# Moving one subtraction per attention item from VectorE to GpSimd in a two-layer transformer kernel

## The reference

```python
# layer 0, attention: 32 query heads, 8 key/value heads of 64, sliding window of 64
qkv = einsum('bsd,od->bso', x, w_qkv)
q, k = rms_norm(q) * q_norm_w, rms_norm(k) * k_norm_w
q, k = rope(q, k)
scores = einsum('bhqd,bhkd->bhqk', q, k_rep) * HEAD_DIM ** -0.5 + sliding_mask
attn = einsum('bhqk,bhkd->bhqd', softmax(scores), v_rep)
out = einsum('bso,do->bsd', attn, w_out)
# layer 0, ffn: weights are int32 with a scale per row, 704 hidden
down(silu(gate(x)) * up(x))
# layer 1: full attention with 16 heads of 16, a rotation of the first 8 channels, no causal mask;
# and a feed-forward block that only the 64 best-ranked tokens of each sequence pass through
```

## Time and profile before

| | before |
|---|---|
| median of 3 runs | 1004.89 us |
| profiled execution | 1006.06 us, its span 1004.3 us |
| TensorE, VectorE busy | 915.7 us, 849.8 us |
| ScalarE, GpSimd busy | 662.2 us, 625.0 us |
| granted TensorE clock | 0.98 of full speed, mean |

### The profile page before, as it was taken

The page is one execution under the profiler, slowest core; times in us unless marked ns, Lnnn a source line. Parts: engine busy times, 40 slices in busy tenths (PEclk is TensorE's granted clock), DMA queues, the critical chain, the costliest instruction groups (busy, mean ns, idle before and its releaser), DMA issues. The chain is left out here.

```text
span 1004.3 us, 26048 instructions
## 1 busy us (share of the span) xinstructions
PE 915.7 (91%) x8671; PEld 500.2 (50%) x8671; DVE 849.8 (85%) x1760; ACT 662.2 (66%) x1747; POOL 625.0 (62%) x891
## 2 busy tenths in 40 slices
PE   4678999999998998999998997599999999999998
PEld 2455666766766766765766765242222222222223
DVE  6898889789789788888888886679999999999961
ACT  3655656556556555555655654128999999998985
POOL 4566668678678678668677766513776676454320
PEclk9899999999999999999999999789999999999999
DMA  7556555444445555445444544332312312413001
GB/s 240 120 100 134 113 95 97 96 93 95 97 90 99 97 86 99 97 92 97 98 88 95 89 87 90 104 92 68 69 27 26 47 27 48 75 40 53 20 5 43
DMA packets 253114, 83.60 MB, mean 83 GB/s; under 512 B 227317, under 2 KB 251573, under 8 KB 252725
## 3 DMA queue, kind: packets, MB, share of 16 engines
q1 hardware_dynamic: 249284, 76.43, 38.2%
q10 hardware_dynamic: 3696, 5.51, 2.0%
HBM read 18.49 MB, written 4.19 MB: 23 GB/s over the span
## 5 line engine op out<-in xcount | busy, mean ns | idle before, releaser
L1342 DVE TENSOR_REDUCE l_mxv<-l_mx 128x1 f32<-128x1024 f32 x256 | 295.0, 1216 | 19.5 <-PE l_mx L1562 19.1
L1262 ACT ACTIVATE l_prob<-l_sc 128x512 f32<-128x512 f32 x512 | 278.3, 598 | 18.3 <-PE l_sc L1570 15.5
L763 POOL TENSOR_TENSOR tt<-tt 128x320 f32<-128x320 f32 x128 | 110.4, 863 | 156.8 <-DVE tt L681 156.8
L420 ACT ACTIVATE an<-an 128x256 f16<-128x256 f32 x128 | 53.4, 417 | 231.9 <-DVE an L616 231.9
L1516 PE MATMUL l_acc<-l_prob,qkv_all 128*17 128x256 f32 x2048 | 161.0, 387 | 2.9 <-DVE l_acc L1325 0.5
L1562 PE MATMUL l_mx<-early 48*128 48x512 f16 x512 | 156.8, 388 | 4.2 <-DVE l_ones L1288 2.6
L754 POOL TENSOR_TENSOR rm<-ss,half_neg 128x5 f32<-128x5 f32 x128 | 159.8, 1248 | 0.0
L1570 PE MATMUL l_sc<-early 50*128 50x512 f16 x512 | 154.8, 383 | 0.1
L884 PE MATMUL qk<-early,xh 128*128 128x384 f16 x512 | 127.9, 332 | 4.8 <-DVE early L565 4.7
L937 PE MATMUL ob<-wo_hi,ats 128*128 128x256 f16 x512 | 105.7, 274 | 6.0 <-DMA ats<-an 4.5
L681 DVE TENSOR_TENSOR tt<-qk,tcw 128x640 f32<-128x640 f32 x128 | 104.4, 816 | 3.7 <-ACT v L420 1.6
(11 more groups left out here) (184 smaller groups left out, 1938.9 us busy)
## 6 DMA issues: line engine op xcount, KB each, us to landing
qkv_all<-w_qkv SPq DMA_DIRECT2D x3, 768.0 KB, 9.2
v<-v SPq DMA_DIRECT2D x64, 32.5 KB, 1.9
xn_all<-xs SPq DMA_DIRECT2D x16, 128.5 KB, 2.1
xa<-x SPq DMA_DIRECT2D x16, 128.0 KB, 2.3
tk<-nat SPq DMA_TRANSPOSE x128, 2.8
qkv_all<-w_o ACTq DMA_DIRECT2D x8, 256.0 KB, 3.1
ats<-an SPq DMA_TRANSPOSE x128, 2.4
xc<-x SPq DMA_DIRECT2D x16, 128.0 KB, 2.3
```

The source lines that it names most:

```text
L420: return act.activation(dst, src, ACT.Copy, scale=scale)
L763: pool.tensor_tensor(t1[:, b, :, :].rearrange("p h (a d) -> p h a d", a=2), t1[:, b, :, :].rearrange("p h (a d) -> p h a d", a=2), tt[:, b ...
L1262: act.activation(prob[:, (y * NI + u) % NPR, h * 512:(h + 1) * 512], sc[:, k % NSC, :], ACT.Exp, scale=D1 ** -0.5).then_inc(s_["act_sc"], 1)
L1342: dve.tensor_reduce(mxv[:, x % 2, u:u + 1], mx[:, MX[k] % 2, :], AX.X, ALU.max).then_inc(s_["dve_mx"], 1)
```

## The change

The subtraction for the low parts of the four queries (`nat[:, b, 2:NB, HD:P]`) leaves VectorE, where it stood behind the key's subtraction at lag 6, and is now issued by GpSimd at lag 5, between the rotation's addition and the power of the item that follows. It waits for ScalarE's high parts (`act_hi`) and, before it writes into `nat`, for the DMA that last read this buffer. What waited for the semaphore `dve_ql` now waits for `pool_lo`: SP's transposing DMA and VectorE's product L681, two items later.

```diff
@@ sync @@
                     sp.wait_ge(s_["dve_kl"], m + 1)
-                    sp.wait_ge(s_["dve_ql"], m + 1)
+                    sp.wait_ge(s_["pool_lo"], m + 1)
@@ vector, at(s, LAG_K) @@
                     dve.tensor_tensor(nat[:, b, 1, 0:HD], t1[:, b, 0, :], nat[:, b, 0, 0:HD], ALU.subtract
                                       ).then_inc(s_["dve_kl"], 1)
-                    dve.wait_ge(s_["act_hi"], n * G + k + 1)
-                    dve.tensor_tensor(nat[:, b, 2:NB, HD:P], t1[:, b, 1:NH, :], nat[:, b, 2:NB, 0:HD], ALU.subtract
-                                      ).then_inc(s_["dve_ql"], 1)
@@ vector, at(s, LAG_A) @@
+                    wait(dve, s_["pool_lo"], n * G + k - 1)
                     wait(dve, s_["dve_kl"], n * G + k - 1)
-                    wait(dve, s_["dve_ql"], n * G + k - 1)
@@ gpsimd, between the rotation's addition and the power @@
+                n, k, ok = at(s, LAG_N)
+                b = k % 2
+                if ok:
+
+                    pool.wait_ge(s_["act_hi"], n * G + k + 1)
+                    landed(pool, n * G + k - 2)
+                    pool.tensor_tensor(nat[:, b, 2:NB, HD:P], t1[:, b, 1:NH, :], nat[:, b, 2:NB, 0:HD], ALU.subtract
+                                       ).then_inc(s_["pool_lo"], 1)
```

More of the change, by code:

```diff
@@ L275, in layer0 @@
                  "act_sq act_A act_kh act_hi act_th act_kc act_kt act_exp act_an act_xh act_xat act_l1 "
-                 "dve_A dve_ss dve_a dve_h dve_rc dve_an dve_al dve_kl dve_ql dve_xl "
+                 "dve_A dve_ss dve_a dve_h dve_rc dve_an dve_al dve_kl dve_xl "
                  "dve_b1 dve_g1 dve_v1 dve_xn dve_x1 dve_b2 dve_g2 dve_v2 dve_xs dve_wr dve_b3 dve_v3 "
                  "dve_xa dve_raw dve_top dve_rest "
-                 "pool_rm pool_u pool_v pool_rs1 pool_rs2 pool_tcw pool_xa "
+                 "pool_rm pool_u pool_v pool_lo pool_rs1 pool_rs2 pool_tcw pool_xa "
                  "pool_r1 pool_r2 pool_rope pool_ones act_wq dve_wq act_wo dve_wo dve_gu dve_wd set_dve set_pool set_k").split()
```

## The result

The changed kernel takes 1010.5 us (median of 22 runs, 1006.63 to 1025.27); the kernel before took 1004.79 in 22 runs beside it. The ratio is 1.0062, 95% interval 1.004 to 1.0084. The profiled execution of the changed kernel took 1011.56 us. In some executions of these kernels TensorE's granted clock stays at 1.2 GHz for 37.5 us between the two layers (e2's trace, from 646.5 us on) and not for 14 us (before, from 647.6 on), which costs about 12 us; so beside the times I compare how far layer 0 has come: the start of the probability matmuls (pv) of item 12 and of item 124, seven periods of 16 items later.

The account below looks back on a forecast made before the run. TensorE was taken as near its limit, with VectorE a second bound alternating within each period. 6.7 periods x (-1.4 + 0.5) = -6.0, head +1, layer 1 and tail 0: -5 us, 1000 on the median; range 992 to 1015.

Parts of the forecast that it names:

- What goes: VectorE loses 128 subtractions, 0.35 us per item; two runs of busy items per period, taken as -1.4 us a period.
- What comes: GpSimd gets 128 subtractions of 0.73 us each (bounds 0.55 and 0.86), making it 89% busy per period.
- rival 3: Shared SBUF port: the key's subtraction on VectorE is held behind GpSimd's new one; +22 us, 1026; chance 0.07.
- The head: From 20 to 100 us, VectorE splitting weights: -4.2 us relief, +5 for blocked weight instructions; taken as +1 us.
- the price of the late place: Behind the layer-1 rotation, once per period, GpSimd runs two microseconds late: +1.0 us, 0.5 absorbed, +0.5 net.
- Mostly ScalarE has room for that: ScalarE's two copies to nat come 0.73 us later per item, claimed mostly harmless as the copy stands last, behind exp.
- three of four items per period stay on time: Argument against rival 1: by the prediction's sums, lateness on GpSimd stays confined to the remaining items of a period.
- About +1.0 us at that sc: TensorE's scores behind the layer-1 rotation: two subtractions add 1.5 us, up to 0.4 taken back; 0.5 then absorbed.
- The moved waits: tk's transpose and VectorE's product two items later now wait for GpSimd; claimed free on time, late only behind the layer-1 rotation.
- Rival 2: Late transposes queue on SP, so the output projection (ob) gets its input up to 1.9 us later; +9, 1014; chance 0.18.
- Rival 1: The place behind the layer-1 rotation costs 1.2 us a period and eats the gain; 1005 to 1006; chance 0.22.
- The sign for "wrong": The prediction would be wrong if, among other signs, the transposes become TensorE's longest wait.

Follow-up runs that it names:

- e2: The changed kernel with the subtraction moved only for items with m % 16 under 12, the others kept on VectorE; 1003.8 us, ratio 1.0006 to the kernel before.
- e3: The kernel before with the queries' subtraction left out on every engine; 990.3 us, ratio 0.9846.
- e17: The kernel before without VectorE's subtraction; GpSimd does it into an unread buffer, tk not waiting, only for items m % 16 under 12; 998.2 us.
- e1: The changed kernel with the subtraction moved only for items with m % 16 of 12 and more; 1012.6 us, ratio 1.0059 to the kernel before.
- e18: The kernel before without VectorE's subtraction; GpSimd does it into an unread buffer, tk not waiting, only for items m % 16 >= 12; 994.6 us.
- e5: The kernel before without VectorE's subtraction; GpSimd does it for all items into an unread buffer and tk's transpose does not wait; 1007.8 us.
- e13: e5 with ScalarE's copy of the carried keys issued one slot earlier, ahead of the copy to nat; 1012.0 us, ratio 1.0041 to the kernel before.
- e6: The changed kernel with GpSimd's subtraction ahead of the rotation's addition; 1037.6 us, ratio 1.0314 to the kernel before.
- e9: e5 with GpSimd's subtraction behind the scaling, not ahead of the power; 1055.3 us, ratio 1.0489 to the kernel before.
- e10: The changed kernel with the moved subtraction behind the next item's scaling; 1069.5 us, ratio 1.0594 to the kernel before.
- e8: The kernel before with the layer-1 rotation's three GpSimd instructions spread over three successive items; 1003.6 us, ratio 0.9964 to the kernel before.
- e14: The changed kernel with ScalarE's copy of the carried keys issued one slot earlier, ahead of the copy to nat; 1017.7 us, ratio 1.0113 to the kernel before.

## Why the prediction was wrong, step by step

It forecast 1000 us, five less than before; the kernel takes five to six more. The range (992 to 1015) holds the time, but its middle rests on a price that failed.

- **"What goes"** was right in sum, by luck. The forecast's relief is 6.7 x 1.4 + 4.2 = 13.6 us, e3 shows 13.57. By place it was off: 1.86 a period (13.03 / 7) and not 1.4, and 0.5 in the head and not 4.2.
- **"What comes", the duration**: 0.72 us against 0.73. L667 (now L664), taken as unchanged, fell by 0.06, and L645 (now L642), which stood only in rival 3, by 0.26.
- **The head**, put at +1: 2.95 by the traces, with the lower clock named above. Its +5 was 8 x 0.65 us of held weight instructions. No run shows the 0.65: for instance the eight instructions that write `wo_lo` rose by 0.10 each (0.76 to 0.86 us), and in e3, with nothing new on GpSimd, by 0.12.
- **The step that failed is the price of the late place**, +1.0 us a period, 0.5 after absorption, with the load on GpSimd at nothing elsewhere. Load and wait cost 2.2 us a period there (the change less e3 in the four items: 2.16 + 0.07), 1.95 of them the load; the net came to +2.16 and not +0.5, while the rest of the period gave 1.52, near the forecast's 1.4. (With the stretch taken one or two items earlier the net is 1.6 or 1.4, and load and wait still cost 2.2 or 2.3.) With the +5 in the head the forecast had 8.4 us of costs; they are 20.3 (15.4 load, 4.9 wait of tk). A period pays 1.96 for the load (13.72 / 7) and 0.45 for the wait. Two sentences stood behind it. "Mostly ScalarE has room for that" is false where nat ends an item's turn and the next item's work queues behind it: the waits for the scaling went from 6 to 44. And "three of four items per period stay on time" counted slack item by item; e17 shows that work put ahead of the block arrives at the block as lateness.
- **"About +1.0 us at that sc", less 0.5 absorbed**: TensorE's wait there grew from 0.70 to 2.12, so 1.4. The two subtractions in the block were 1.4 us as forecast, but the 0.4 that an earlier product should take back did not come: with the relief alone (e3) this wait is 0.91 and not 0.70, since TensorE is there earlier and GpSimd's block is not shorter. And the exp wait that should absorb some had gone with the relief already; behind it came 1.88 for the next transpose, where it was 0.52. The upper bound of 1.9 net is just passed by the 2.16.
- **The moved waits**: VectorE's product waits 1.44 us in each of the six late places and nowhere else from 100 to 603 us, as forecast. "On time both cost nothing" holds by e2 against e17, as far as single traces tell. The relief taken as equal per item, e2's three quarters cost 0.75 x 13.03 - 3.98 = 5.8 us with the wait, and e17's 6.0 without. In the late quarter the same sum gives 8.3 with it (e1) and 5.8 without (e18): the wait costs 2.5 us there.
- **Rival 3 (port)** is refuted for this kernel: L603 stayed at 0.38, far under the 0.8 named. **Rival 2** (1014; 1007 to 1018 holds the time) had the sign and the late transposes, but not the wait that it charged: that of ob did not grow (3.1 to 1.7), that of the scores did. **Rival 1** named the place that eats the gain, with too small a price (1.2 us a period).
- The sign for "wrong" that the prediction named last came true: the transposes are TensorE's longest wait. VectorE's busy time fell by 43.6 and not 54; the prediction's own 0.33 us from start to start gives 128 x 0.33 = 42, since busy time counts overlapping instructions once.

What is shown: relief and load as separate sums; that the load's cost meets in the late place and passes through ScalarE's queue behind nat (e5, e13). The size of the wait of tk is read from single traces. What stays open: whether a place in GpSimd's queue exists that delays neither the scaling nor VectorE's product, since e6, e9 and e10 each brought their own wait; and whether leaving out the items just ahead of the layer-1 rotation too would turn e2 into a gain. The best of the kernels that do the whole work is e8, which moves nothing and only spreads the layer-1 rotation (0.9964 [0.9933, 0.9996]).

## What to carry to other kernels

Price an instruction added to an in-order queue not by the mean slack of its items but at the longest unbroken block of that queue: work put into the block delays its end, and so did work put just ahead of it. Then ask who waits for that engine, and what stands behind the waiting instruction in its queue, since moving one item of that queue away only brings the next to the front. Two experiments size such a move before it is made: leave the work out (the most it can bring), and put it on the new engine, writing to a buffer that nobody reads (what it costs; the engines that overwrite its inputs must still wait for it).

## What was not expected of the hardware

A short stop of TensorE can cost more than itself. In the changed kernel it stands 2.34 us before the scores at 542.62, and then the granted clock (the third column from the end) falls, from the windows view:

```profile
542.00:543.00 1.00, 0.38 (x4) 0.37 (x5) 0.89 (x4) 0.56 (x4) 1.00 (x3) 1.00 0.65 131
543.00:544.00 1.00, 1.00 (x8) 0.58 (x6) 0.48 (x2) 1.00 (x5) 1.00 (x1) 0.66 0.44 134
544.00:545.00 1.00, 1.00 (x6) 0.83 (x4) 1.00 (x2) 0.78 (x3) 0.92 (x3) 0.50 0.47 89
...
546.00:547.00 1.00, 1.00 (x18) 0.81 (x15) 0.15 (x1) 0.00 (x0) 1.00 (x2) 0.64 0.64 126
547.00:548.00 1.00, 1.00 (x9) 0.66 (x8) 0.80 (x4) 0.47 (x2) 1.00 (x2) 1.00 0.13 33
```

TensorE is busy throughout and runs at 1.2 GHz for 0.68 + 1 + 1 + 0.72 = 3.4 us: 1.7 us of work lost. It does not happen each time: the changed kernel stood over 2 us six times between 100 and 603 us, and the clock fell after two of them; in e5 it fell after four of six such stops, in e3, e17 and e18, whose stops up to 603 us stay at 1.71 or less, never. The shortest stop with such a fall behind it is one of 1.80 us in e14 (at 317.01). e13 had five such falls up to item 124 and e14 four, so a part of what they lost may be this. So a period in which e5 loses the clock costs 2.2 us more than in e3, and one in which it doesn't 1.3 (starts of items 24, 40 and so on to 120 in the two traces; four and two periods). That is some 3.6 us of e5's 13.7 if the fall is the only difference between the two kinds of period, and e17's and e18's 0.75 each, by the same starts, make 1.5 together, near the 1.3 and under e5's mean of 1.93. No forecast that sums waits one by one has this term.
